# A two-layer decoder on one core: the first loads cut into parts, the context transposed later, and the fp4 weights quantised in three parts between the streams' steps

## The reference

```python
x = _layernorm(x + _L0_attn_ref(x, Wq, Wk, Wv, Wo))          # causal self-attention, 16 heads of 8, rotary
x = _layernorm(x + _L0_xattn_ref(x, ctx_1024, ...))          # attention to the context, q and k layer-normed per head
x = _layernorm(x + _L0_ffn_ref(x, w_gate, w_up, w_down))     # gated FFN of 352, fp4 (blocks of 16)
x = _layernorm(x + _L1_attn_ref(x, ...))                     # linear-attention block with depthwise convolutions and an MLP
x = _layernorm(x + _L1_xattn_ref(ctx_1024, x, ...))          # causal attention to the context
x = _layernorm(x + _L1_ffn_ref(x, ...))                      # 8 experts of 256, the best two per token
```

```python
xb = x.reshape(shape[:-1] + (shape[-1] // BLOCK, BLOCK))
scale = jnp.maximum(jnp.max(jnp.abs(xb), axis=-1, keepdims=True) / 6.0, 1e-12)
xn = xb / scale
q = _GRID[jnp.searchsorted(_MID, jnp.abs(xn))] * jnp.sign(xn) * scale
```

## Time and profile before

| what | value |
|---|---|
| median of 3 runs | 747.43 us (747.34 to 751.6) |
| the profiled execution | 747.63 us |
| its span, first to last instruction | 745.8 us |
| mean granted TensorE clock | 0.848 of 2.4 GHz |
| busy: TensorE, VectorE, ScalarE, GpSimd | 557.3, 532.0, 326.2, 203.9 us |
| instructions | 13887 |

### The profile page before, as it was taken

One profiled execution on the slowest core, in us unless ns is written; L12 is line 12 of the kernel. 1 busy time (PEld: TensorE's weight loads), 2 busy tenths in 40 slices (PEclk: granted clock), 3 DMA queues, 4 the chain that ended last, 5 costly groups with the idle time before them and its releaser, 6 DMA issues.

```text
span 745.8 us, 13887 instructions
## 1 busy us (share of the span) xinstructions
PE 557.3 (75%) x4864; PEld 389.2 (52%) x4864; DVE 532.0 (71%) x1520; ACT 326.2 (44%) x637; POOL 203.9 (27%) x316
## 2 busy tenths in 40 slices
PE   5697668666488869687885696566888797789954
PEld 3466536434255337454674364354453375687841
DVE  7877777898758667657776678987676676765734
ACT  1653345322275556115633462222864551354631
POOL 4304300201100620274024011021016112774533
PEclk9997669888789989769977697976999795699987
DMA  9993100000000000020000000000000000332324
GB/s 293 324 296 108 29 0 2 1 1 0 2 0 1 1 1 2 1 80 14 2 2 0 1 2 1 0 2 0 1 1 0 1 3 1 89 115 71 84 88 115
DMA packets 45555, 32.34 MB, mean 43 GB/s; under 512 B 4280, under 2 KB 43456, under 8 KB 45360
## 3 DMA queue, kind: packets, MB, share of 16 engines
q1 hardware_dynamic: 43216, 26.54, 12.8%
q0 software_dynamic: 2272, 4.92, 1.9%
HBM read 13.83 MB, written 17.62 MB: 42 GB/s over the span
## 4 chain that ended last, share of the span: by engine, by line
PE 46%; DVE 33%; ACT 9%; issue 6%; POOL 2%; DMA 2%; DVEq 0%; SPq 0%; POOLq 0%; ACTq 0%
PE ps L624 5%; PE ps L605 5%; PE ps L668 5%; PE ps L943 5%; PE ps L957 2%; DVE s_row_max L1344 2%; DVE s_probs L1349 2%; ACT s_probs L1084 2%; PE ps L874 2%; PE ps L869 2%; DVE s_r L1313 2%; PE ps L636 2%; DVE s_work L1303 1%; DVE s_work L1300 1%; DVE s_work L1290 1%
## 5 line engine op out<-in xcount | busy, mean ns | idle before, releaser
L1883 POOL TENSOR_TENSOR s_rs<-s_mv,eps 128x1 f32<-128x1 f32 x80 | 16.4, 207 | 347.0 <-DVE s_mv L1319 346.9
L1344 DVE TENSOR_REDUCE s_row_max<-ps 128x16 f32<-128x1024 f32 x48 | 58.7, 1222 | 41.6 <-PE ps L624 41.4
L605 PE MATMUL ps<-tabs,s_probs 128*128 128x128 f32 x384 | 63.2, 295 | 17.1 <-ACT s_probs L1084 15.8
L1064 ACT ACTIVATE s_pT<-ps 128x512 f32<-128x512 f32 x96 | 55.6, 594 | 39.0 <-PE ps L605 38.5
L624 PE MATMUL ps<-s_k,s_q 64*64 64x256 f32 x768 | 61.0, 442 | 9.9 <-ACT s_q L1034 9.9
L605 PEld LDWEIGHTS ps<-tabs,s_probs 128*128 128x128 f32 x384 | 44.2, 148 | 37.7 <-ACT s_probs L1084 25.7
L1084 ACT ACTIVATE s_probs<-s_probs 128x1024 f32<-128x1024 f32 x48 | 50.6, 1056 | 24.5 <-DVE s_probs L1349 24.5
L1349 DVE TENSOR_TENSOR s_probs<-ps,s_row_max 128x1024 f32<-128x1024 f32 x48 | 58.7, 1222 | 1.3
L668 PE MATMUL ps<-s_v,s_pT 128*64 128x18 f32 x1536 | 56.2, 218 | 4.1 <-ACT s_headsT L1075 1.9
L668 PEld LDWEIGHTS ps<-s_v,s_pT 128*64 128x64 f32 x1536 | 52.4, 146 | 11.8 <-issue 11.0
L943 PE MATMUL ps<-s_pT,s_k 128*128 128x128 f32 x312 | 44.5, 287 | 4.6 <-issue 2.8
(11 more groups left out here) (285 smaller groups left out, 1262.9 us busy)
## 6 DMA issues: line engine op xcount, KB each, us to landing
rows_io<-zero_rows SPq DMA_DIRECT2D x9, 1152.0 KB, 11.9
s_probs<-rows_io SPq DMA_DIRECT2D x39, 72.0 KB, 1.9
s_cin<-in_ctx SPq DMA_DIRECT2D x4, 256.0 KB, 3.7
s_xin<-in_x SPq DMA_DIRECT2D x4, 256.0 KB, 4.3
wgu<-in_wg SPq DMA_DIRECT2D x1, 1024.0 KB
wgu<-in_wu SPq DMA_DIRECT2D x1, 1024.0 KB
wo<-in_wo SPq DMA_DIRECT2D x1, 1024.0 KB
s_probs<-shares_io SPq DMA_DIRECT2D x4, 256.0 KB, 5.2
```

The lines of the kernel that those rows point to most:

```text
L605: ins = pe.transpose(h.ps[:, 2, tile(j)], h.probs[:, t % 2, 8 * part + 2 * j:8 * part + 2 * j + 2, :] .rearrange("p h k -> p (h k)"), ident)
L1064: act.activation(h.pT[:, t % 2, 4 * part:4 * part + 4, :].rearrange("p j q -> p (j q)"), h.ps[:, 2, :], ACT.Copy).then_inc(h.pT_here.sem, 1)
L1344: dve.tensor_reduce(h.row_max[:, t % 2, :], s3, AX, ALU.max).then_inc(h.max_here.sem, 1)
```

## The change

SP loads the tables in two pieces (the identity and the rotary tables first: TABLES is reordered for that) and the first matrices as four and two. The order of the queue is now: first tables, x of stream 0, four matrices, fp4_d, x of stream 1, the other tables, the two matrices of the values and the output, the mask, fp4_gu, small tables, both contexts, the other matrices. The waits on tabs_here, mats_here and mask_here are joined by v_mats_here and more_tabs_here.

The context is no longer transposed at the start of a stream's pass. turn_context on TensorE and take_context on ScalarE do it after the scores of the fourth tile of the self-attention, one step before keys_ahead, which now waits for it. This holds in both passes.

ffn_weights becomes a part of the third woven program on VectorE: three parts of nine operations (fp4_d, the first half of fp4_gu, the second half, 128x384 each), in place, with gu_w and d_w as scratch, and after them next_row, taken and ids. The table ORDER sets where each operation stands. It is a new table for all engines.

```diff
@@ -78,3 +78,3 @@
 
-TABLES = [("ident", P), ("rope", P), ("diag", P), ("cos_q", S), ("sin_q", S), ("cos_k", S), ("sin_k", S),
+TABLES = [("ident", P), ("cos_q", S), ("sin_q", S), ("cos_k", S), ("sin_k", S), ("rope", P), ("diag", P),
           ("head", H), ("member", GH), ("side", 2), ("iota", EXPERTS), ("first_row", EXPERTS), ("ids", 2 * TILES),
@@ -88,3 +88,4 @@
 HEADS_NORM, ROTATED = 17, 4
-MATS_FIRST = 6
+
+TABS_FIRST, MATS_FIRST, MATS_THEN = P + 4 * S, 4, 6
 
 ORDER = {
     "pe": (
-        0, 1, 0, 3, 2, 0, 1, 1, 0, 1, 1, 0, 1, 1, 0, 3, 3, 0, 3, 1, 0, 1, 1, 0, 2, 1, 0, 1, 1, 0, 2, 1, 0,
...
+        0, 1, 0, 2, 1, 0, 1, 1, 0, 2, 2, 0, 2, 2, 0, 1, 1, 0, 4, 3, 0, 5, 2, 0, 7, 4, 0, 2, 2, 0, 1, 3, 0,
...
@@ -454,2 +456,4 @@
         more_mats_here = sem("more_mats_here")
+        v_mats_here = sem("v_mats_here")
+        more_tabs_here = sem("more_tabs_here")
         mask_here = sem("mask_here")
@@ -488,3 +492,3 @@
 
-        WEIGHTS_ONCE = 18
+        WEIGHTS_ONCE = 27
         block = ctx.enter_context(nc.Block())
@@ -498,4 +502,6 @@
 
-            def load(c, k):
+            def load_context(c, k):
                 sp.dma_start(streams[k].cin[:, :, :], tiles(ctx_in, c, k)).then_inc(streams[k].c_here.sem, 16)
+
+            def load_x(c, k):
                 sp.dma_start(streams[k].xin[:, :, :], tiles(x_in, c, k)).then_inc(streams[k].x_here.sem, 16)
@@ -541,13 +547,17 @@
 
-            sp.dma_start(fp4_gu[:, :], fp4_gu_in.rearrange("p c n -> p (c n)")).then_inc(fp4_here, 16)
-            sp.dma_start(tabs[:, :], tables_in).then_inc(tabs_here, 16)
-            load(0, 0)
+            sp.dma_start(tabs[:, 0:TABS_FIRST], tables_in[:, 0:TABS_FIRST]).then_inc(tabs_here, 16)
+            load_x(0, 0)
             sp.dma_start(mats[:, 0:MATS_FIRST, :], mats_in[:, 0:MATS_FIRST, :]).then_inc(mats_here, 16)
             sp.dma_start(fp4_d[:, :], fp4_d_in).then_inc(fp4_d_here, 16)
-            load(0, 1)
+            load_x(0, 1)
+            sp.dma_start(tabs[:, TABS_FIRST:], tables_in[:, TABS_FIRST:]).then_inc(more_tabs_here, 16)
+            sp.dma_start(mats[:, MATS_FIRST:MATS_THEN, :], mats_in[:, MATS_FIRST:MATS_THEN, :]).then_inc(v_mats_here, 16)
             sp.dma_start(identb[:, :], identb_in).then_inc(mask_here, 16)
             sp.dma_start(cmask[:, :], cmask_in).then_inc(mask_here, 16)
+            sp.dma_start(fp4_gu[:, :], fp4_gu_in.rearrange("p c n -> p (c n)")).then_inc(fp4_here, 16)
             sp.dma_start(cols[:, :], cols_in).then_inc(cols_here, 16)
             sp.dma_start(ranks[:, :], ranks_in).then_inc(mask_here, 16)
-            sp.dma_start(mats[:, MATS_FIRST:, :], mats_in[:, MATS_FIRST:, :]).then_inc(more_mats_here, 16)
+            for k in range(STREAMS):
+                load_context(0, k)
+            sp.dma_start(mats[:, MATS_THEN:, :], mats_in[:, MATS_THEN:, :]).then_inc(more_mats_here, 16)
             sp.dma_start(bp[:, :], bp_in.partition_broadcast(P)).then_inc(biases_here, 16)
@@ -567,3 +577,4 @@
                     sp.wait_ge(*h.summed.at(TILES, c - 1))
-                    load(c, k)
+                    load_x(c, k)
+                    load_context(c, k)
                 for k, h in enumerate(streams):
@@ -583,2 +594,7 @@
                         pe.wait_ge(*h.x_new.at((sub - 1) * TILES + t + 1))
+                    elif t == 0:
+                        pe.wait_ge(*h.x_here.at(16))
+                        if h.turn:
+                            pe.wait_ge(*h.route_act.at(0))
+                            pe.wait_ge(*h.route_dve.at(0))
                     ins = pe.transpose(h.ps[:, bank, tile(t)], src[:, t, :], ident)
@@ -681,2 +697,10 @@
 
+            def turn_context(h):
+                yield
+                pe.wait_ge(*h.c_here.at(16))
+                pe.wait_ge(*h.shifted.at(TILES))
+                for t in range(TILES):
+                    ins = pe.transpose(h.ps[:, 0, tile(t)], h.cin[:, t, :], ident)
+                ins.then_inc(h.ct_turned.sem, 1)
+
             def keys_ahead(h):
@@ -685,2 +709,3 @@
                 pe.wait_ge(more_mats_here, 16)
+                pe.wait_ge(*h.ct_here.at(1))
                 pe.wait_ge(*h.shifted.at(TILES))
@@ -697,11 +722,2 @@
             def self_attention(h):
-                yield
-                pe.wait_ge(*h.x_here.at(16))
-                pe.wait_ge(*h.c_here.at(16))
-                if h.turn:
-                    pe.wait_ge(*h.route_act.at(0))
-                    pe.wait_ge(*h.route_dve.at(0))
-                for t in range(TILES):
-                    ins = pe.transpose(h.ps[:, 0, tile(t)], h.cin[:, t, :], ident)
-                ins.then_inc(h.ct_turned.sem, 1)
                 yield from turn_x(h, 0, h.xin, 3)
@@ -711,3 +727,2 @@
                 pe.wait_ge(*h.xt_here.at(1))
-                pe.wait_ge(*h.ct_here.at(1))
                 pe.matmul(h.ps[:, 0, 0:TOK], mat("a0_q"), h.xT[:, :], start=True, stop=True)
@@ -718,2 +733,3 @@
                 pe.wait_ge(*h.q_here.at(1))
+                pe.wait_ge(v_mats_here, 16)
                 values(h, h.xT, "a0_v", 0)
@@ -723,3 +739,3 @@
                 pe.wait_ge(mask_here, 48)
-                yield from attention_tiles(h, 0, 0, True, "a0_o", {1: keys_ahead})
+                yield from attention_tiles(h, 0, 0, True, "a0_o", {0: turn_context, 1: keys_ahead})
                 yield from turn_heads(h, 1)
@@ -1015,2 +1031,7 @@
 
+            def take_context(h):
+                yield
+                act.wait_ge(*h.ct_turned.at(1))
+                act.activation(h.cT[:, :], h.ps[:, 0, 0:TOK], ACT.Copy).then_inc(h.ct_here.sem, 1)
+
             def take_values(h, n, bank):
@@ -1031,2 +1052,4 @@
                 yield
+                if n == 0 and h.turn == 0:
+                    act.wait_ge(more_tabs_here, 16)
                 act.wait_ge(*h.q_here.at(n + 1))
@@ -1088,8 +1111,2 @@
             def self_attention(h):
-                yield
-                if h.turn:
-                    act.wait_ge(*h.route_pe.at(0))
-                    act.wait_ge(*h.route_dve.at(0))
-                act.wait_ge(*h.ct_turned.at(1))
-                act.activation(h.cT[:, :], h.ps[:, 0, 0:TOK], ACT.Copy).then_inc(h.ct_here.sem, 1)
                 yield from take_x(h, 1, 3)
@@ -1098,3 +1115,3 @@
                 yield from take_values(h, 0, 0)
-                yield from attention_tiles(h, 0, None, {2: lambda h: square_heads(h, 1)})
+                yield from attention_tiles(h, 0, None, {0: take_context, 2: lambda h: square_heads(h, 1)})
                 yield from gain_heads(h, 1, h.kT, h.k_here)
@@ -1264,3 +1281,2 @@
 
-            act.wait_ge(tabs_here, 16)
             weave((network(first), network(second), blocks_of_experts()), ORDER["act"])
@@ -1270,8 +1286,7 @@
         def _(dve):
-            def quantize(h, src, dst, blocks, sig, count):
+            def quantize(h, src, dst, blocks, sig, count, places=None):
 
                 n = blocks * BLOCK
-                v, e = h.qv[:, 0:n], h.qe[:, 0:n]
+                v, e, m, rc = places or (h.qv[:, 0:n], h.qe[:, 0:n], h.qmax[:, 0:blocks], h.qrcp[:, 0:blocks])
                 v3 = v.rearrange("p (b k) -> p b k", k=BLOCK)
-                m, rc = h.qmax[:, 0:blocks], h.qrcp[:, 0:blocks]
 
@@ -1494,12 +1509,20 @@
 
-            def ffn_weights(h):
-                gu3 = fp4_gu[:, :].rearrange("p (b k) -> p b k", k=BLOCK)
-                ins = yield from quantize(h, gu3, gu3, 2 * KC * P // BLOCK, once, 0)
-                ins.then_inc(once.sem, 1)
-                dve.wait_ge(*once.at(9))
-                dve.wait_ge(fp4_d_here, 16)
-                d3 = fp4_d[:, :].rearrange("p (b k) -> p b k", k=BLOCK)
-                ins = yield from quantize(h, d3, d3, FFN_PAD // BLOCK, once, 9)
-                ins.then_inc(once.sem, 1)
-                dve.wait_ge(*once.at(WEIGHTS_ONCE))
+            def ffn_weights():
+
+                for n, (w, here) in enumerate(((fp4_d[:, :], fp4_d_here), (fp4_gu[:, 0:FFN_PAD], fp4_here), (fp4_gu[:, FFN_PAD:], fp4_here))):
+                    blocks, room = FFN_PAD // BLOCK, d_w[:, :, :].rearrange("p c n -> p (c n)")
+                    w3 = w.rearrange("p (b k) -> p b k", k=BLOCK)
+                    yield
+                    dve.wait_ge(here, 16)
+                    if n:
+                        dve.wait_ge(*once.at(9 * n))
+                    ins = yield from quantize(None, w3, w3, blocks, once, 9 * n, (w, gu_w[:, 0:FFN_PAD], room[:, 0:blocks], room[:, blocks:2 * blocks]))
+                    ins.then_inc(once.sem, 1)
+                yield
+                dve.wait_ge(more_tabs_here, 16)
+                dve.tensor_copy(next_row[:, :], tab("first_row")).then_inc(once.sem, 1)
+                dve.memset(taken[:, :], 0.0).then_inc(once.sem, 1)
+                for k, h in enumerate(streams):
+                    dve.tensor_scalar(h.ids[:, :, :].rearrange("p k t -> p (k t)"), tab("ids"), float(TOK * (k - STREAMS)), None,
+                                      ALU.add).then_inc(once.sem, 1)
 
```

(13 more changed lines are left out.)

## The result

The changed kernel takes 764.01 us (median of 4 runs, 761.85 to 764.98) where the kernel before takes 749.48 on the same chip: a ratio of 1.019, 95% interval 1.014 to 1.024. The forecast was 744.7 in 738.0 to 749.5, so the change is slower by 14.5 us where I expected 2.7 us less. The profiled execution took 764.98 us.

What follows compares the result with a forecast made beforehand. No engine was full (TensorE 75%, VectorE 71% of 745.8 us); VectorE ended last at the start. -7.3 + 4.6 + 0.5 - 0.5 = -2.7 on 747.6 gave 744.9, 744.7 as a median; range 738 to 749.5.

Steps and rivals of the forecast that it cites:

- The start: Up to the first maximum: earlier loads and moved quantising bring it from 27.96 to 20.7 us, -7.3.
- The quantising: Self-attention: operations between maxima and subtractions take 6.3 us of VectorE, 1.7 fill free time, +4.6.
- My bound of +6.3: Upper bound of the quantising's cost in the self-attention, when none of VectorE's 2.8 free us is filled.
- The order elsewhere: Rest of the kernel: streams keep their distance to within some operations, so 0, bounds -3 and +3.
- The sign of being wrong that the text named: The prediction is wrong if stages behind 60 us take another time than before; no size given.
- The FFN, for which the weights are needed, comes after 100 us: Ground for costing the later weights at nothing, each load or value being there 5 us or more before use.
- The context: Transposes and copy moved to the self-attention's tail: +0.5 in the first pass, -0.5 in the second.
- rival 3: Self-attention tails: key projection waits for context transposes and copy, 4.8 in place of 0.5; 748.4 us, chance 0.12.
- (1): Self-attention: quantising hidden whole, the start's 7.3 us gain lives on; 739.6 us, chance 0.20.
- (2): GpSimd's key spreads hold VectorE's moved operations, 1.6 us each for one or two; 746.3 to 747.9 us, chance 0.12.
- (4): Start: loads not earlier in proportion, stream 1's x at 9.2, 2.5 us lost; 747.2 us, chance 0.09.
- slower by over 1%: Whole kernel over 754.9 us, needing rival 3 and a bad order together; chance 0.04.

Runs made afterwards that it cites:

- e1: The changed kernel with the last of the 27 quantising operations moved right behind the 26th on VectorE, in the self-attention; 761.64 us, ratio 1.018.
- e11: The changed kernel with twelve dummy transposes added on TensorE ahead of its wait at 28 us, run on another chip; ratio 1.023.
- e8: e2 with fourteen dummy transposes added on TensorE ahead of its wait for stream 1's second tile; 750.44 us, ratio 1.0025.
- e3: e2 with the 18 operations that quantise fp4_gu moved from the self-attention into VectorE's idle stretches of the cross-attention; 744.5 us, ratio 0.9935.
- e2: e1 with both streams' steps in the order of the kernel before; only the context's steps stand in the tail; 754.87 us, ratio 1.007.
- e5: The changed kernel, new order throughout, with the 18 operations on fp4_gu in the cross-attention as in e3; 763.1 us, ratio 1.015.
- e10: e1 with the order of the kernel before only between about 95 and 190 us of the first pass; 757.18 us, ratio 1.011.
- e9: e3 with dummy transposes on TensorE ahead of its waits for stream 0's x, stream 1's x and stream 1's first scores; 740.82 us, ratio 0.989.
- e6: e3 with the context's steps at the start of each pass and the contexts loaded right behind the second x; 747.4 us, ratio 0.997.
- e4: e1 with the streams' steps in the order of the kernel before from about 95 us on; 751.49 us, ratio 1.002.
- e12: The changed kernel run again unchanged, on another chip; ratio 1.024.

## Why the prediction was wrong, by its steps

- **The start (-7.3).** Right in mechanism: -6.2. Stream 0's x landed at 4.3 as forecast, fp4_d at 7.2 for 5.6, stream 1's x at 7.9 for 6.7, and the first projections ran at the low clock (1.92 and 1.29), which the text had named as its doubt. The rotary product at 11.86 lies within its bounds (5 to 7.4 us earlier). How well the size fits is in part luck: the same order had its first maximum anywhere from -6.5 to -4.7 (e1, e11), as the second projection took 1.17 to 1.91.
- **The quantising (+4.6).** VectorE's own share, 3.5 in the old order (e8 against e3, at 68 us), is near the 4.6. Missing was that a full VectorE empties TensorE, and that TensorE then comes back at half clock: 5.5 more in e2 at 68 us. My bound of +6.3 "when none is" filled took the operations' time as the most that they can cost. VectorE at 17.4 and TensorE at 16.6 of 20.2 us already said that both were nearly the bound; what delays one idles the other. In the new order, which is the one forecast, the term is small: e1 is 1.6 us above e5 by the ratios and 1.5 below it by the medians, so no cost of the 18 operations beside the order's can be told from nothing.
- **The order elsewhere (0, bounds 3 either way).** This is the step that failed by most. "The streams keep their distance to within some operations" was read from how far apart the streams are. The order alone costs 16.4 us by the ratios of e5 and e3. The price is in single rows: 5.9 us in the self-attention by stream 0's centring (4.8 by stream 1's, e5), 6.2 by two rows of 128x16 and 128x128 that stand behind one quantising and a half of stream 0's x (e1, e10), 3.3 in the MLP, 3.8 in the same block of the second pass. That is 18 to 19 us, more than the changed kernel's whole 17.4. The sign of being wrong that the text named, other times for the stages behind 60 us, is what the table shows (+1.5 at 68 us, +17.4 at the end).
- **"The FFN, for which the weights are needed, comes after 100 us", at nothing.** The weights are used there, but they are asked for in row 120 of TensorE's order, and their last operation stood in row 217 of VectorE's. Both rows were there to be read. That it cost 0.4 us by itself and not 5.47 (e1) is luck: the next wait was as long.
- **The context (+0.5, -0.5).** In the first pass small, as forecast: e9 loses 0.2 across the tail (from -6.8 to -6.6), and rival 3's wait is not in its trace. e3 against e6 has the later context worth 2.3 at the first maximum and 0.9 at 58 us. The second pass's -0.5 is not shown: there the difference of the two kernels comes back to 0.9 at 412 us after 1.2 at 256.
- **Rivals.** (1) "Hidden whole" came true only where I had not looked for it, in the idle stretches of the cross-attention (e3). (2) No quantising operation took over 1 us. Beside GpSimd's second spread, one with two operands at 22.90 took 0.55 as without it, and one at 24.50 took 0.59 where e3 has 0.36: 0.2 us at most. By the rule of the Trainium skill that the text had drawn on (SBUF — State Buffer, section SBUF: two separate sides) the first of them would have been held; the trace does not show it. (3) See the context. (4) The loads came 1.2 to 1.6 us later than forecast, no more, and TensorE started at 4.3.
- **The chances.** 0.04 for slower by over 1% rested on the order being worth 3 us at most. Four tables with some 1700 numbers, new as a whole, have no row of the trace, and a bound of 3 us for them had no reason.

## What to carry to other kernels

When an order table is replaced, read for each engine's waits at what row the awaited operation now stands on its own engine, row by row against before; the distance of the streams says little. A filler belongs where its engine waits for something that is long in coming (a chain of small steps of the other stream), not between two operations that take turns with another engine. And when a wait is found in a profile, the next one behind it must be looked for before a price is put on it.

## What the runs showed of the hardware

- TensorE's granted clock fell to half after stretches in which it had little to do, and the work after them was then slow for some 7 us: 0.29 of 3 us busy, then a clock of 0.61, 0.50 and 0.75 (e2). Fourteen dummy transposes in that gap kept it at 1.00 and made the kernel 3.4 to 4.4 us faster; in e9 twenty-three of them brought 3.7. Not every such stretch brought it down: in e5 TensorE was busy 1.59 of 3 us from 30 to 33, and the clock stayed at 1.00. The Trainium skill (TensorE: Matmul & The Clock Gate, section HAM oscillation — how this bites in real kernels) describes waits for a DMA that bring the clock down and the work behind them starting slow; here the wait was for another engine, and the traces agree on what follows, 1.92 us for the 16 score matmuls that take 1.03 otherwise.
- The granted clock is shown as 1.00 from the start of every trace, but the first projections of e3 at 9 to 12 us take 1.92 us, as at half clock, and 1.02 in e9, where TensorE had worked before. In the first microseconds the durations tell the clock, the column does not.
- The same order gave different clocks in the same place (e1, e4 and e10: +0.3, +2.9 and +1.9 at 94 us), and in another kernel the same to 0.2 us on two chips (the changed kernel and e12).
